# Fifteen extra TensorE matmuls around the h2n turns of a language-model tower

## The reference

```python
h = tok(x, emb0..3, proj0..3)                       # 4096 tokens x 256
h = h + attn(layernorm(h), ...)                     # conv, state-space scan, gate, w2
h = h + ffn(layernorm(h), ...)                      # shared gated MLP + two hash-routed experts

def attn(x):
    x_conv = silu(depthwise_conv(x @ w1_w.T + w1_b))
    return ssm(x_conv) * silu(x @ v1_w.T + v1_b) @ w2_w.T + w2_b

def ffn(x):
    shared = silu(x @ sw1 + sb1) * (x @ sw3 + sb3) @ sw2 + sb2
    for k in range(2):                              # expert of token n: (11 n + 7919 k) % 8
        out[idx] += gelu(x[idx] @ w1[e] + b1[e]) @ w2[e] + b2[e]
    return (shared + out / 2) / 2
```

## Time and profile before

| | us |
|---|---|
| median of 3 runs | 440.75 |
| lowest, highest | 439.66, 442.76 |
| the profiled execution | 440.18 |
| span of its profile | 438.3 |
| outside the span | 1.88 |
| mean granted TensorE clock | 0.992 |

### The profile page before, as it was taken

The page is one execution under the profiler, slowest core; times in us unless marked ns, Lnnn a source line. Parts: engine busy times, 40 slices in busy tenths (PEclk is TensorE's granted clock), DMA queues, the critical chain, the costliest instruction groups (busy, mean ns, idle before and its releaser), DMA issues.

```text
span 438.3 us, 8454 instructions
## 1 busy us (share of the span) xinstructions
PE 399.5 (91%) x2880; PEld 351.6 (80%) x2880; DVE 272.8 (62%) x607; ACT 243.5 (56%) x435; POOL 211.5 (48%) x236
## 2 busy tenths in 40 slices
PE   3869999899998874999999999999999999998996
PEld 2858788788677863788898988988988888897885
DVE  6667998889756778464565565564554654655333
ACT  4567777768887436635535635635635536435442
POOL 6578988831005555648337247247247336433000
PEclk9999999999999989899999999999999999999999
DMA  2424111249699982101111211201301301100101
GB/s 63 145 80 161 49 58 57 65 129 323 182 312 303 239 314 96 50 0 49 53 45 48 59 40 49 84 11 48 96 0 49 96 0 49 48 0 0 49 0 48
DMA packets 32779, 38.86 MB, mean 89 GB/s; under 512 B 3461, under 2 KB 29027, under 8 KB 32624
## 3 DMA queue, kind: packets, MB, share of 16 engines
q1 hardware_dynamic: 29616, 32.99, 24.3%
q0 software_dynamic: 3136, 5.52, 4.1%
HBM read 34.56 MB, written 8.65 MB: 99 GB/s over the span
## 4 chain that ended last, share of the span: by engine, by line
PE 65%; DVE 15%; POOL 6%; ACT 6%; issue 4%; DMA 3%; DVEq 0%; SPq 0%; ACTq 0%; POOLq 0%
PE ps L1152 20%; PE ps L1153 20%; PE ps L1154 20%; DVE hid_lo L1085 3%; DMA h_in<-h_rows_dram 2%; DVE stat L963 2%; POOL bias_e L657 1%; POOL bias_e L658 1%; PE ps L1160 1%; PE ps L1271 1%; PE ps L1190 1%; DVE x_mid L1016 1%; DVE act_out L1079 1%; ACT act_out L857 1%; DVE catT_lo L956 1%
## 5 line engine op out<-in xcount | busy, mean ns | idle before, releaser
L1085 DVE SCALAR_TENSOR_TENSOR hid_lo<-act_out,hid_hi 128x512 fp32r<-128x512 f32 x64 | 54.4, 851 | 57.6 <-ACT hid_hi L870 57.6
L857 ACT ACTIVATE act_out<-ps,vec 128x512 f32<-128x512 f32 x32 | 22.0, 689 | 90.5 <-PE ps L1154 90.5
L1079 DVE SCALAR_TENSOR_TENSOR act_out<-ps,vec,act_out 128x512 f32<-128x512 f32 x32 | 24.0, 751 | 55.6 <-ACT act_out L857 55.6
L687 POOL TENSOR_TENSOR h_sb<-h_sb,bias_e 128x256 f32<-128x256 f32 x32 | 24.5, 769 | 53.6 <-DVE h2n L976 53.6
L1154 PE MATMUL ps<-h2nT_hi,sw_lo 128*128 128x512 f32 x128 | 50.0, 391 | 0.0
L1153 PE MATMUL ps<-h2nT_lo,sw_hi 128*128 128x512 f32 x128 | 50.0, 391 | 0.0
L1152 PE MATMUL ps<-h2nT_hi,sw_hi 128*128 128x512 f32 x128 | 49.9, 390 | 0.0
L680 POOL TENSOR_TENSOR zc_lo<-v_sb,zc_hi 128x256 fp32r<-128x256 f32 x32 | 28.9, 907 | 34.4 <-ACT zc_hi L847 34.4
L861 ACT ACTIVATE act_out<-ps,vec 128x512 f32<-128x512 f32 x32 | 22.1, 689 | 40.4 <-PE ps L1154 40.3
L537 POOL DMA_INDIRECT cat<-table_dram,x_ids x32 | 35.7, 1115 | 8.4 <-issue 5.8
L870 ACT ACTIVATE hid_hi<-act_out 128x512 fp32r<-128x512 f32 x64 | 39.7, 622 | 0.0
(11 more groups left out here) (133 smaller groups left out, 1254.2 us busy)
## 6 DMA issues: line engine op xcount, KB each, us to landing
toep_l<-kernel_rows_dram SPq DMA_DIRECT2D x14, 512.0 KB, 9.0
toep_r<-kernel_rows_dram SPq DMA_DIRECT2D x12, 512.0 KB, 6.4
h_rows_dram<-h_ring SPq DMA_DIRECT2D x32, 128.0 KB, 1.8
h_in<-h_rows_dram SPq DMA_DIRECT2D x8, 512.0 KB, 4.5
stage<-w_e_dram POOLq DMA_DIRECT2D x7, 512.0 KB, 3.6
out_dram<-o_sb SPq DMA_DIRECT2D x7, 512.0 KB, 3.2
bias_e<-rows_dram SPq DMA_DIRECT2D x1, 1024.0 KB, 7.3
toep_r<-kernel_rows_dram SPq DMA_DIRECT2D x4, 256.0 KB, 7.7
```

The lines of the kernel that those rows point to most:

```text
L687: nc.gpsimd.tensor_tensor(at, at, bias_e[:, bass.ds(e, 1), :].rearrange("p o c -> p (o c)"), ALU.add).then_inc(h2_biased, 1)
L857: nc.scalar.activation(act_out[:, n % 4, :], ps[bank][:, :], ACT.Silu, bias=vec[:, C_SB1 + j:C_SB1 + j + 1]).then_inc(act_done, 1)
L1079: nc.vector.scalar_tensor_tensor(act_out[:, n % 4, :], ps[bank + 1][:, :], vec[:, C_SB3 + j:C_SB3 + j + 1], act_out[:, n % 4, :], ALU.add, ...
L1085: nc.vector.scalar_tensor_tensor(hid_lo[:, n % 4, :], act_out[:, n % 4, :], 0.5 if kind == SHARED else 0.25, f32(hid_hi[:, n % 4, :]), ALU ...
```

## The change

A helper issues matmuls of 512 columns (both halves of `w2_hi` moving, its first 128 columns as weights) into `ps[2]`, which nothing reads. It waits for nothing and signals nothing. Three are issued ahead of each of the four turns of slot 0, and three ahead of slot 0: fifteen in all. The other engines' programs are the same.

```diff
+        def keep_awake(times):
+
+            for _ in range(times):
+                nc.tensor.matmul(ps[2][:, :], w2_hi[:, 0, 0:P], w2_hi[:, :, :], start=True, stop=True)
+
...
         for g in range(GROUPS):
             mixer_mm(0, g)
         for g in range(GROUPS):
+            keep_awake(3)
             mixer_turn(0, g)
+        keep_awake(3)
         slot(0, 0, True, False)
```

## The result

The changed kernel runs in 439.05 us (median of 22 executions, 437.52 to 440.4) against 440.5 us (22 executions, 438.93 to 442.8) for the kernel before: ratio 0.9969, 95% interval 0.9956 to 0.9981. That is 1.37 us less (0.84 to 1.94). The profiled execution took 438.7 us, its span is 436.8.

The account below looks back on a forecast made before the run. TensorE, busy 91% of the span, was taken as the bound. A 1.04 us gain from the held clock and 0 for the groups gave 439.14 from 440.18, or 439.71 from 440.75; forecast 439.4, range 438.0 to 441.6.

Parts of the forecast that it names:

- The clock: In 171.6 to 175.1 us, TensorE busy about 2.7 us instead of 0.88, so full clock holds through to slot 0.
- The cost of the groups: Added matmuls ahead of the turns and slot 0 fit into TensorE's waits; cost 0, bounds 0 to 0.54 us.
- the cover: At turn 0: 0.16 us between its results being ready (170.85) and VectorE taking them up (171.01), hiding its 0.54 us delay.
- The first unit: Slot 0's first expert matmuls at full clock: the seventh starts at 176.94, 1.27 us earlier.
- GpSimd is late next: Ahead of slot 1's mixer matmul, GpSimd's load issue, free at 178.75, limits the gain to 1.04 us instead of 1.27.
- Nothing lost later: After that mixer matmul TensorE has no idle time and ScalarE and VectorE move along, so the 1.04 us stays.
- rival 2: The clock holds, but the gain is taken back in slot 0; 440.3 to 440.7 us, chance 0.14.
- The sum: Whole kernel: 440.18 - 1.04 + 0 = 439.14, or 439.71 from the median of three; forecast between them, 439.4 us.
- rival 1: Ahead of slot 0 the clock falls all the same, nothing gained or paid; about 440.6 us, chance 0.14.
- Rival 3: Groups run at half clock, 1.28 us each, and slot 0 starts 1.4 us late; 441.6 us, chance 0.10.

Follow-up runs that it names:

- e1: Changed kernel with the fifteen added matmuls cut from 512 to 32 columns, number and places kept; ratio to the kernel before 0.9991.
- e8: Changed kernel with only the group of three matmuls right ahead of slot 0 left; ratio to the kernel before 1.0001.
- e3: Changed kernel with six instead of three matmuls in each of the five groups; ratio to the kernel before 1.0015.
- e6: e4_pool_later plus a GpSimd wait, behind the load issue, for VectorE's first hid_lo of slot 0; ratio to the kernel before 0.9969.
- the repeat: The changed kernel itself measured once more, nothing altered; 438.6 us, ratio to the kernel before 0.9975.
- e4_pool_later: Changed kernel with GpSimd's wait for the low parts and expert load issue moved behind its first zc_lo; ratio to the kernel before 1.0021.
- e5_pool_only: Kernel before, without added matmuls, with only GpSimd's wait and load issue moved behind mixer_lo(1, 0); ratio to the kernel before 1.0001.

## Why the prediction was right

The forecast was 439.4 us within 438.0 to 441.6, and within 1%; measured were 439.05 and a ratio of 0.9969. By its steps:

- *The clock.* It held through to slot 0, in both profiles of the change. The busy time for 171.6 to 175.1 was forecast as about 2.7 and is 2.32. The sum added records whole, but a turn's record of 0.44 overlaps the group behind it, which starts 0.20 later, and group 3 had ended at 171.6, since this execution runs 0.43 us ahead of the one before; moved by that, the stretch 171.17 to 174.67 has 2.53. The side on which it lies was right by a smaller margin than the step claimed, and the step took it from two rows of one execution. e1 and e8 show that the clock does fall when there is less.
- *The cost of the groups.* Turn 0 came 0.82 us after the last mixer matmul instead of 0.27, 0.55 late (forecast 0.54). Turn 1 stood 1.74 behind it instead of 1.67. VectorE took up the first turned group at 170.59, 1.86 behind the last mixer matmul against 1.81, so the cover held but for 0.05. Turns 2 and 3 came at 3.43 and 4.96 instead of 3.39 and 4.92, and slot 0 at 6.32 instead of 6.28. Taking 0 was right to 0.04. e3 shows what the cover is worth: past it, the turns cost their full time.
- *The first unit.* The seventh matmul started 1.51 us behind the first, forecast 1.46, before 2.73: a gain of 1.22, not 1.27. The first step is 0.35, not 0.31.
- *GpSimd is late next.* Its load issue stands 2.65 us behind slot 0's start in both profiles (178.13 - 175.48 and 177.70 - 175.05), zc_lo follows at 3.30 (forecast 3.28), and TensorE's mixer matmul at 4.21 (forecast 4.17). The gain is 1.00 us, forecast 1.04, and TensorE's wait there grew to 1.16. e6 confirms the cap by taking it away.
- *Nothing lost later.* The rest is 257.5 against 257.6 us, and TensorE's next waits of over half a microsecond are the same in both (0.61 at 201.71 and 0.59 at 208.36; before at 203.18 and 209.83), so rival 2 is out.
- *The sum.* The measured 1.37 us has an interval of 0.84 to 1.94; the repeat's ratio of 0.9975 gives 1.1 (0.5 to 1.7). Both hold 1.04, and so does the piece's 1.00. Whether the mean gain is above the piece's these numbers do not settle. That the forecast of 439.4 came within 0.35 of the median is partly luck: it started between one execution (440.18) and the median of three (440.75). The median of 22 is 440.5, and 440.5 - 1.04 is 439.46. What the prediction did not see is how mild its one execution was. It reckoned with one stay of 3.4 us at half clock taken away; over many executions of the kernel before and of the change it is about 6 us, and how much of that lies on the path is open.
- *Rivals.* The clock falling all the same (rival 1) was seen only with fewer or narrower matmuls. Rival 3, the groups at half clock, was seen in part: in e3 the first group ran at half clock behind a fall at 168.7, over the mixer matmuls. It did not show in either profile of the change. The prediction had it as unlikely and gave as a reason that the clock was high in 161.4 to 171.6; that was true of one execution, and three of the ten other profiles have a fall there (at 165.5, 166.0 and 168.7).

## What to carry to other kernels

Where an engine works in short bursts between waits and then starts dense work at a lower clock, wide matmuls into a free bank are a cheap cure if they fit the waits: add up waits and groups one by one, and spread them, since three right ahead of the dense work did not hold the clock here. Expect a small gain: here a quarter to a third of a per cent. It is less than the clock's whole price, because the chain moves to whatever did not depend on it; look for that release first (here 0.3 us on GpSimd). When the effect is a microsecond and the scatter three, cut the profiles at fixed instructions and compare the pieces, and read the mean granted clock of all executions to learn whether a profile is typical.

## What was not expected of the hardware

- A VectorE instruction of 0.7 us took 5.32 while GpSimd ran four tensor operations back to back (e4_pool_later), and cost the kernel 2.4 us (the rest of 260.0 against 257.6). Making GpSimd wait 0.67 us for it removed the stall (e6_pool_yields).
- The moments at which TensorE's clock falls differ from execution to execution of like code: over the mixer matmuls in three of the profiles, not in the other nine; around the start of slot 0 at 175.1 in the kernel before, at 174.4 in e1_narrow, at 173.6 in e8_last_one, at 175.8 in e5_pool_only. In e1_narrow it stayed at 1.2 GHz to 181.2, 6.8 us, although TensorE was busy for 2.72 us of the first 3.4.
